# Row numbers of a counting stage in the result memory, node groups every three steps, and one-hot rows by ScalarE

## The chip, the cores and the metric

The kernel runs on one core of one Trainium2 chip. The metric is the device time of one execution in microseconds; every number below is of this core. Its engines are TensorE (matrix products, into a result memory of eight banks of 512 float32 values per partition), VectorE, ScalarE, GpSimd (here mostly the issuer of indirect DMAs, gathers and scatters by row number) and SyncE (the issuer of the plain DMAs).

## The reference

Four graph layers run one after another on the same 50,000 nodes of 128 features and 25,000 edges (`src`, `dst`, `dst` sorted), each followed by a residual and a layer norm:

```python
x = _layernorm(x + _L0_gnn_ref(x, node_vec, edge_weight, edge_attr_128, ...))   # attention with time encoding
x = _layernorm(x + _L1_gnn_ref(x, L1_gnn_W1, ...))      # two hidden convolutions and an output one
x = _layernorm(x + _L2_gnn_ref(x, edge_attr_128, src, dst, ...))    # two layers with edge rows and a mean
x = _layernorm(x + _L3_gnn_ref(x, edge_attr_2, src, dst, ...))      # attention over edges, two features
```

A convolution gathers `h[src]`, scales, adds up over equal `dst`, and multiplies by a 128x128 weight. An edge's sums only reach its own `dst`; a node without an incoming edge gets dense work alone (products, layer norms), which needs no gather. The result is a float32 table of 50,000 x 128.

## The kernel before

The edges are put in slots: 196 tiles of 128 (`TILES`), taken in 49 groups of four tiles (`GROUPS`, K = 4, G = 512). The 50,000 nodes are 98 groups of 512. The program is a sequence of blocks; each block has one list of instructions per engine, all engines meet at its end, and inside it only semaphores order them. The blocks that matter here:

1. **Counting** (L292 to L372). GpSimd issues 196 gathers of one tile each (L324: rows of x with one more value) into a ring of six, and SyncE writes each finished group to `xs0_d`. Beside it, with no semaphore between the two, VectorE makes one-hot rows by comparing the row of numbers 0 to 390 (`lanes`) with each edge's node number split in a low part (128 values) and a high part (391 values): four `tensor_tensor` operations a group in `equal` (L356 to L366), two of 128x512 and two of 128x1564. TensorE multiplies low and high one-hots into two banks `c_ps`, which are counts per node. The block ends when both strands have.
2. **Table and ranking** (to about 740 us): a short block turns counts into start positions, then each edge gets its slot, with 196 scatters (L528).
3. **Attention of layer 0**, and **the dense stage** (L1571 on, 107 steps): groups 0 to 48 are edge groups, then `NN` node groups. `dense_pe`, `dense_act` and `dense_dve` take each group through a pipeline of ten steps. GpSimd looks up 196 tiles of a table meanwhile, spread evenly over the steps, after VectorE's signal of each step.
4. **Four convolution blocks** (`conv_hidden` twice, the third convolution, `conv_edges`), with 55, 55, 57 and 54 steps (`STEPS_H`, `STEPS_T`, `STEPS_E`); a step takes a group of 512 edges: four gathers (L1919), scaling, a transpose, the segmented scan (L1938), products, and stores. In these blocks run also the **node passes**: the node groups 0 to `FILLED` - 1 are not in the dense stage but are done here, one pass after another, with instructions placed between those of the convolutions by a step counter T that runs on through all four blocks:

```python
FILLED = (2 * STEPS_H + STEPS_T + STEPS_E - 22) // 4 + 1
def node_of(T, phase):
    j, late = divmod(T - phase, 4)
    return j if late == 0 and 0 <= j < FILLED else -1
```

A pass has phases -3 to 21: load of x (-3), transpose of x (0), copy (1), product (2), squares (3), first root (4), y (5), transpose of y (7), copy (8), products (9, 12), and so on to the second norm (14, 16, 17, 19, 20) and the store (21). `fill_sp`, `fill_pe`, `fill_act_early`, `fill_act` and `fill_dve` issue them. The two transposes share the bank `fa_ps`.

5. **Fifth convolution** (`conv_edges` with `final`): 60 steps, no passes.
6. **Last one-hot rows** (L2521 on): SyncE broadcasts 49 rows of 512 lane numbers into a ring of six (`lane_b`); VectorE compares each with the partition's own number (L2591), TensorE multiplies the one-hots of a tile by a 128x196 table, VectorE picks one value a row (L2597). Then short work in rows, and the last block with the scatter of the results.

## Time and profile before

| | us |
|---|---|
| median of 3 runs | 4391.33 |
| their range | 4370.59 to 4411.52 |
| the profiled execution | 4386.8 |
| its span, first to last instruction | 4385.1 |

The median and the profiled execution are different executions of the same program. Times of the trace count from the span's start. Engines in the rows: PE is TensorE's products, PEld its weight loads, DVE VectorE, ACT ScalarE, POOL GpSimd; a q behind a name is that engine's sequencer. The buffer number is left out of a name, so `xs` stands for `xs0`, `x_f` for several tiles, `c_ps` for two banks.

### The profile page before, as it was taken

The numbers are of one execution on the slowest core, as the hardware profiler recorded it, in microseconds if no ns is written. First come the engines' busy times: TensorE is split into PE (matmuls) and PEld (weight loads), VectorE is DVE, ScalarE is ACT, GpSimd is POOL, SyncE is SP. The second block draws the span as 40 slices with busy tenths as digits, with TensorE's granted clock in tenths as the row PEclk, the third lists the DMA queues.
The fourth block names the chain that finished last, engine by engine and source line by source line (L and its number), as shares of the span: only waits on it lengthen the run. The fifth ranks groups of instructions, "written<-read, shape, count | busy, mean of one in ns | idle before, by whom it ended". The sixth has DMA issues, their size and how long they took to land. (4 is left out here: it accounts for less than half of the span.)

```text
span 4385.1 us, 57861 instructions
## 1 busy us (share of the span) xinstructions
PE 2745.6 (63%) x14955; PEld 2056.1 (47%) x14955; DVE 2776.3 (63%) x7991; ACT 1897.4 (43%) x5652; POOL 2119.6 (48%) x1978
## 2 busy tenths in 40 slices
PE   4514875599677776896467567555646646778422
PEld 1102443366355555674355456433445546776321
DVE  8914997344597999996245455566735436778533
ACT  0001332377323666797355355455734435660111
POOL 8874554566001222332755566455265545630466
PEclk7656998699799888998788777777767777888555
DMA  2233554677297444332355466555555556753221
GB/s 59 58 92 104 152 154 131 162 245 240 78 326 241 135 135 135 95 102 93 115 160 167 153 193 203 174 179 183 161 173 178 176 184 190 230 160 121 72 72 59
DMA packets 532622, 662.42 MB, mean 151 GB/s; under 512 B 99720, under 2 KB 300998, under 8 KB 532296
## 3 DMA queue, kind: packets, MB, share of 16 engines
q1 hardware_dynamic: 466440, 557.83, 40.2%
q0 software_dynamic: 65856, 100.90, 8.7%
q8 instruction: 125, 2.05, 0.2%
q14 instruction: 201, 1.65, 0.1%
HBM read 441.09 MB, written 246.14 MB: 157 GB/s over the span
## 5 line engine op out<-in xcount | busy, mean ns | idle before, releaser
L1919 POOL DMA_INDIRECT xg_c<-r_d,src_row x392 | 417.2, 1064 | 304.2 <-issue 114.8
L1593 POOL DMA_INDIRECT look<-table_d,ids x196 | 196.7, 1004 | 720.1 <-DVEq L1569 689.6
L324 POOL DMA_INDIRECT xs<-in_x_vec,node_i x196 | 294.2, 1501 | 61.1 <-issue 61.1
L1938 DVE TENSOR_TENSOR_SCAN agg_t_c<-flags_c,agg_t_c,t_ps_c 128x512 f32<-128x512 bf16 x144 | 183.6, 1275 | 191.9 <-remote 182.8
L2666 POOL DMA_INDIRECT out<-x_f,out_row x196 | 196.8, 1004 | 221.7 <-DVE x_f L2732 162.0
L1919 POOL DMA_INDIRECT xg_c<-x2d_d,src_row x196 | 198.6, 1013 | 215.9 <-DMA xg_c<-x2s_d 158.2
L528 POOL DMA_INDIRECT rows_d<-row,slot_i x196 | 194.7, 993 | 190.0 <-DVEq L590 142.3
L1919 POOL DMA_INDIRECT xg_c<-x1d_d,src_row x196 | 206.2, 1052 | 166.0 <-DMA xg_c<-x1s_d 107.1
L1919 POOL DMA_INDIRECT xg_c<-g1d_d,src_row x196 | 201.6, 1029 | 160.7 <-DMA xg_c<-g1s_d 100.3
L903 POOL DMA_INDIRECT xd<-in_x,ids x196 | 205.4, 1048 | 104.1 <-issue 52.9
L1998 PE MATMUL m_ps_c<-w_L_gnn_Wr,term_t_c 128*128 128x128 f32 x784 | 129.7, 318 | 200.8 <-issue 111.0
L1938 DVE TENSOR_TENSOR_SCAN agg_t_c<-flags_c,agg_t_c,term_t_c 128x512 f32<-128x512 bf16 x96 | 122.9, 1281 | 208.9 <-remote 139.9
L1998 PEld LDWEIGHTS m_ps_c<-w_L_gnn_Wr,term_t_c 128*128 128x128 f32 x784 | 114.5, 224 | 212.7 <-issue 117.1
L2683 PE MATMUL f_ps<-e2n,mean_in 2*128 2x128 f32 x392 | 97.5, 430 | 158.5 <-DVE y_f L2716 120.0
L623 PE MATMUL a_ps<-run,lo_t 128*128 128x391 f32 x392 | 175.5, 530 | 2.4
L359 DVE TENSOR_TENSOR hot_hi<-lanes,part_f 128x1564 bf16<-128x1564 f32 x98 | 174.3, 1779 | 0.0
L633 ACT ACT_TABLE_LOAD x1 | 1.3, 1283 | 387.1 <-PEq L399 387.1
L2683 PEld LDWEIGHTS f_ps<-e2n,mean_in 2*128 2x128 f32 x392 | 86.6, 324 | 169.5 <-issue 168.0
L2324 PE MATMUL z_ps_c<-w_L_gnn_W,agg_t_c 128*128 128x128 f32 x784 | 131.8, 307 | 52.8 <-issue 52.2
L1051 DVE SCALAR_TENSOR_TENSOR prod_t<-kv_ps,b_k,q_t 128x512 f32<-128x512 f32 x49 | 36.8, 751 | 193.2 <-issue 97.2
L2321 PE MATMUL z_ps_c<-w_L_gnn_W,own_t_c 128*128 128x128 f32 x784 | 136.1, 315 | 33.0 <-issue 32.5
L2017 ACT COPY term_t_c<-t_ps_c 128x512 f32<-128x512 f32 x98 | 57.1, 583 | 228.5 <-remote 203.4
(478 smaller groups left out, 9253.4 us busy)
## 6 DMA issues: line engine op xcount, KB each, us to landing
flags_c<-cont_d SPq DMA_DIRECT2D x245, 128.0 KB
xm<-rows_d SPq DMA_DIRECT2D x49, 512.0 KB
m_d<-m_c SPq DMA_DIRECT2D x98, 256.0 KB
r_d<-r_c SPq DMA_DIRECT2D x98, 256.0 KB
m_in_c<-m_d SPq DMA_DIRECT2D x98, 256.0 KB
e_c<-rows_d SPq DMA_DIRECT2D x98, 256.0 KB
x_f<-in_x SPq DMA_DIRECT2D x50, 256.0 KB
out<-x_f SPq DMA_DIRECT2D x50, 256.0 KB
```

The source lines that it names most:

```text
L324: pool.indirect_dma_start(out=xs0[:, h, k, :], out_offset=None, in_=a["x_vec"][:, :], in_offset=bass.IndirectOffsetOnAxis(ap=node_i[:, 1, ...
L359: return dve.tensor_tensor(to, number[:, 0:width].unsqueeze(1).to_broadcast([P, K, width]), same, ALU.is_equal)
L528: pool.indirect_dma_start(out=rows_d[:, :], out_offset=bass.IndirectOffsetOnAxis(ap=slot_i[:, h, k:k + 1], axis=0), in_=row[:, h, k, :], i ...
L623: pe.matmul(a_ps[u % 2][:, 0:HI], lo_t[:, u % 3, :], run[:, u % 3, :], start=True, stop=True).then_inc(based.sem, 1)
L903: pool.indirect_dma_start(out=xd[:, s, k, :], out_offset=None, in_=a["x"][:, :], in_offset=bass.IndirectOffsetOnAxis(ap=ids[:, 1, t:t + 1] ...
L1593: pool.indirect_dma_start(out=look[:, t, :], out_offset=None, in_=table_d[:, :], in_offset=bass.IndirectOffsetOnAxis(ap=ids[:, 0, t:t + 1] ...
L1919: pool.indirect_dma_start(out=xg[:, s, k, :], out_offset=None, in_=table, in_offset=bass.IndirectOffsetOnAxis(ap=src_row[:, t:t + 1], axis=0),
L1938: dve.tensor_tensor_scan(agg_t[:, n % 2, :], flags[:, n % SL, :], terms, agg_t[:, (n - 1) % 2, G - 1:G] if n else 0.0, ALU.mult, ALU.add). ...
L1998: mm = pe.matmul(m_ps[:, chunk(k)], term_t[:, n % 2, chunk(k)], weights[w_side][:, :], start=True, stop=True)
L2321: pe.matmul(z_ps[n % 2][:, chunk(k)], own_t[:, n % 3, chunk(k)], weights[w_own][:, :], start=k == 0, stop=False, skip_group_check=True)
L2666: pool.indirect_dma_start(out=out[:, :], out_offset=bass.IndirectOffsetOnAxis(ap=out_row[:, t:t + 1], axis=0), in_=x4[:, n % SF, k, :], in ...
L2683: mm = pe.matmul(f_ps[n % 3][:, chunk(k)], mean_in[:, n % SF, chunk(k)], e2n[:, :], start=True, stop=True)
```

## The change

Three parts. In the counting stage a bank `lanes_ps` of the result memory gets a copy of the numbers 0 to 390, and the four comparisons of a group read that in place of `lanes`. Node passes begin every three steps, not four, so `FILLED` grows and `NN` shrinks by the same number; some buffers of a pass get one more slot, two rows of x are loaded at step 0, waits on earlier passes are set accordingly, and in `fill_dve` phase 19 is placed ahead of phase 16 (both now fall into the same step). In the last one-hot stage ScalarE makes the rows, as |lane number - own number| and then relu(1 - that), and VectorE keeps only the picks.

```diff
+                lanes_ps = bank(ps, "lanes_ps")
...
                     dve.tensor_copy(lanes[:, :], lanes_i[:, :]).then_inc(steps_v.one(), 1)
+                    dve.tensor_copy(lanes_ps[:, 0:HI], lanes_i[:, :]).then_inc(steps_v.one(), 1)
...
                         same = part_f[:, s, t:t + K].unsqueeze(2).to_broadcast([P, K, width])
-                        return dve.tensor_tensor(to, number[:, 0:width].unsqueeze(1).to_broadcast([P, K, width]), same, ALU.is_equal)
+                        return dve.tensor_tensor(to, lanes_ps[:, 0:width].unsqueeze(1).to_broadcast([P, K, width]), same, ALU.is_equal)
...
-        FILLED = (2 * STEPS_H + STEPS_T + STEPS_E - 22) // 4 + 1
+        FILLED = (2 * STEPS_H + STEPS_T + STEPS_E - 22) // 3 + 1
...
-            y2_f = sb("y2_f", [P, 3, K, D], F32, st_f)
+            y2_f = sb("y2_f", [P, 4, K, D], F32, st_f)
-            u_f = sb("u_f", [P, 2, K, D], F32, st_f)
+            u_f = sb("u_f", [P, 3, K, D], F32, st_f)
-            rest_f = sb("rest_f", [P, 3, K], F32, st_f)
+            rest_f = sb("rest_f", [P, 4, K], F32, st_f)
...
-                j, late = divmod(T - phase, 4)
+                j, late = divmod(T - phase, 3)
...
-                j = 0 if T == 0 else max(node_of(T, -3), 0) if node_of(T, -3) > 0 else -1
-                if j >= 0:
+                for j in range(2) if T == 0 else range(node_of(T, -3), node_of(T, -3) + 1) if node_of(T, -3) > 0 else ():
...
-                    pe.wait_ge(f_xt.sem, f_xt.at(min(j + 2, FILLED)))
+                    pe.wait_ge(f_xt.sem, f_xt.at(min(j + 3, FILLED)))
...
-                    if j >= 2:
-                        pe.wait_ge(f_yt.sem, f_yt.at(j - 1))
+                    if j >= 3:
+                        pe.wait_ge(f_yt.sem, f_yt.at(j - 2))
...
+            apart_of = sb("apart_of", [P, 2, G], F32, st)
+            minus_lane = sb("minus_lane", [P, 1], F32, st)
...
-                            sp.wait_ge(hot_made.sem, hot_made.at(n - SZ + 1))
+                            sp.wait_ge(apart_made.sem, apart_made.at(n - SZ + 1))
...
                 def _(act):
+                    act.wait_ge(minus_ready.sem, minus_ready.at(1))
+                    for it in range(GROUPS + 1):
+                        n = it
+                        if n < GROUPS:
+                            act.wait_ge(lane_in[n % SZ].sem, lane_in[n % SZ].at(n // SZ + 1))
+                            if n >= 2:
+                                act.wait_ge(hot_made.sem, hot_made.at(n - 1))
+                            act.activation(apart_of[:, n % 2, :], lane_b[:, n % SZ, :], ACT.Abs, bias=minus_lane[:, 0:1]).then_inc(apart_made.sem, 1)
+                        n = it - 1
+                        if 0 <= n < GROUPS:
+                            if n >= 3:
+                                act.wait_ge(picks.sem, picks.at(K * (n - 2)))
+                            act.wait_ge(apart_made.sem, apart_made.at(n + 1))
+                            act.activation(one_hot[:, n % 3, :], apart_of[:, n % 2, :], ACT.Relu, bias=ones[:, 0:1], scale=-1.0).then_inc(hot_made.sem, 1)
...
-                    for n in range(GROUPS + 1):
-                        if n < GROUPS:
-                            dve.wait_ge(lane_in[n % SZ].sem, lane_in[n % SZ].at(n // SZ + 1))
-                            if n >= 3:
-                                dve.wait_ge(picks.sem, picks.at(K * (n - 2)))
-                            dve.tensor_scalar(one_hot[:, n % 3, :], lane_b[:, n % SZ, :], lane[:, 0:1], None, ALU.is_equal).then_inc(hot_made.sem, 1)
-                        if n >= 1:
-                            for t in range((n - 1) * K, n * K):
...
+                    for t in range(TILES):
+                        dve.wait_ge(picks.sem, picks.at(t + 1))
```

## Rows read from the trace of the kernel before

**Rows 1.** The page, part 1: busy time, share of the span, instructions

```profile
PE 2745.6 (63%) x14955; PEld 2056.1 (47%) x14955; DVE 2776.3 (63%) x7991; ACT 1897.4 (43%) x5652; POOL 2119.6 (48%) x1978
```

**Rows 2.** Stretches: length, PE, PEld, DVE, ACT, POOL busy, PEclk, DMA share, GB/s

```profile
100.00:150.00 50.00, 27.39 (x87) 9.90 (x87) 50.00 (x44) 0.00 (x0) 43.30 (x23) 0.60 0.24 56
...
2068.00:2430.00 362.00, 219.14 (x1363) 177.66 (x1363) 152.04 (x340) 169.80 (x518) 206.25 (x196) 0.79 0.49 153
2430.00:2800.00 370.00, 238.58 (x1428) 193.30 (x1428) 203.68 (x469) 190.97 (x583) 227.69 (x210) 0.76 0.60 190
...
3175.00:3560.00 385.00, 232.49 (x1428) 202.18 (x1428) 183.01 (x384) 164.96 (x479) 198.46 (x196) 0.73 0.58 176
3560.00:3950.00 390.00, 256.86 (x1742) 242.99 (x1743) 240.25 (x781) 216.32 (x587) 201.62 (x196) 0.76 0.63 193
```

**Rows 3.** GpSimd in time, counting stage: start, duration, line, idle before

```profile
8.30 1.17 POOL L324 DMA_INDIRECT xs<-in_x_vec,node_i  x1 [1.73 <-issue]
...
100.95 1.99 POOL L324 DMA_INDIRECT xs<-in_x_vec,node_i  x1 [0.30 <-issue]
...
241.25 1.00 POOL L324 DMA_INDIRECT xs<-in_x_vec,node_i  x1 [0.30 <-issue]
...
360.88 1.00 POOL L324 DMA_INDIRECT xs<-in_x_vec,node_i  x1 [0.30 <-issue]
```

**Rows 4.** TensorE in time, first product of the block after counting

```profile
370.41 1.64 PE L414 MATMUL tot_ps<-count,ones 128*128 128x391 f32 x2 [127.81 <-PEq L292]
```

**Rows 5.** VectorE in time, counting stage, two successive wide one-hots

```profile
100.31 1.78 DVE L359 TENSOR_TENSOR hot_hi<-lanes,part_f 128x1564 bf16<-128x1564 f32 x1
...
102.61 1.78 DVE L359 TENSOR_TENSOR hot_hi<-lanes,part_f 128x1564 bf16<-128x1564 f32 x1
```

**Rows 6.** VectorE in time, dense stage, one node group to the next

```profile
1900.93 0.69 DVE L1485 TENSOR_TENSOR half_u<-nu_ps,lk_n 128x512 f32<-128x512 f32 x1
...
1901.74 0.69 DVE L1491 TENSOR_TENSOR u_n<-y_n,half_u 128x512 f32<-128x512 f32 x1
...
1906.22 0.69 DVE L1485 TENSOR_TENSOR half_u<-nu_ps,lk_n 128x512 f32<-128x512 f32 x1
```

**Rows 7.** A gather and a scan in time, first convolution

```profile
2238.53 1.93 POOL L1919 DMA_INDIRECT xg_c<-x1d_d,src_row  x1 [0.30 <-issue]
```

```profile
2238.37 1.28 DVE L1938 TENSOR_TENSOR_SCAN agg_t_c<-flags_c,agg_t_c,term_t_c 128x512 f32<-128x512 bf16 x1 [7.68 <-remote]
```

**Rows 8.** The page, part 5: the scatters of the ranking stage

```profile
L528 POOL DMA_INDIRECT rows_d<-row,slot_i x196 | 194.7, 993 | 190.0 <-DVEq L590 142.3
```

**Rows 9.** Groups of instructions, 2068 to 3560: busy us, mean ns, idle before

```profile
L1823 ACT ACTIVATE x_f<-u_f,shift_f,inv_f 128x128 f32<-128x128 f32 x200 | 82.5, 492 | 2.4 <-issue 1.2 <-DVE shift_f L1884 1.1
...
L1845 DVE SCALAR_TENSOR_TENSOR y_f<-fm_ps,inv_f,b_mid 128x128 f32<-128x128 f32 x200 | 56.3, 345 | 2.0 <-issue 0.3
...
L1876 DVE SCALAR_TENSOR_TENSOR sp_f<-mom_f,rest_f 128x4 f32<-128x4 f32 x50 | 8.1, 162 | 1.7
```

**Rows 10.** VectorE and TensorE in time, last one-hot stage

```profile
3990.77 0.49 DVE L2591 TENSOR_SCALAR one_hot<-lane_b,lane 128x512 f32<-128x512 f32 x1
3991.17 0.42 DVE L2597 SCALAR_TENSOR_TENSOR picked<-tile_no,src_tile,pz_ps 128x196 f32<-128x196 f32 x1
...
3991.74 1.56 PE L2553 MATMUL pz_ps<-attn_in,one_hot 128*128 128x196 f32 x8 [0.19 <-DVE picked L2597]
...
3992.52 0.49 DVE L2591 TENSOR_SCALAR one_hot<-lane_b,lane 128x512 f32<-128x512 f32 x1
```

**Rows 11.** ScalarE in time, first convolution: a square from SBUF

```profile
2250.03 0.65 ACT L1800 ACTIVATE sq_f<-y_f 128x512 f32<-128x512 f32 x1
```

**Rows 12.** ScalarE in time, third convolution: two successive copies of x

```profile
3034.07 0.59 ACT L1784 COPY xt_f<-fa_ps 128x512 f32<-128x512 f32 x1 [9.99 <-remote]
...
3063.63 0.58 ACT L1784 COPY xt_f<-fa_ps 128x512 f32<-128x512 f32 x1 [10.10 <-remote]
```

**Rows 13.** Waits, fifth convolution (3570 to 3950): us, times, longest

```profile
POOL xg_c L1919 <- DMA xg_c<-g1s_d: 69.9, 16, 14.1
```

More of the change, by code:

```diff
@@ L365, in _ @@
                         for s, low in ((0, low_of[:, t:t + K, :]), (1, hot_lo[:, h:h + K, :])):
-                            equal(low, lanes, P, 2 * s, t)
-                            equal(hot_hi[:, s, h:h + K, 0:HI], lanes, HI, 2 * s + 1, t).then_inc(hot_ready.sem, 1)
+                            equal(low, P, 2 * s, t)
+                            equal(hot_hi[:, s, h:h + K, 0:HI], HI, 2 * s + 1, t).then_inc(hot_ready.sem, 1)
                     dve.wait_ge(hot_used.sem, hot_used.at(TILES))
@@ L1822, in fill_act @@
                     for k in range(K):
-                        made = act.activation(x4_f[:, j % 2, k, :], u_f[:, j % 2, k, :], ACT.Identity,
+                        made = act.activation(x4_f[:, j % 2, k, :], u_f[:, j % 3, k, :], ACT.Identity,
                                               bias=shift_f[:, j % 2, k:k + 1], scale=inv2_f[:, j % 2, k:k + 1])
@@ L1862, in fill_dve @@
                     dve.tensor_tensor(flat(half_f[:, :, :]), fn_ps[:, :], flat(lk_f[:, :, :]), ALU.max).then_inc(f_halved.sem, 1)
[L1863 to L1864 removed]
+                    if j >= 3:
+                        dve.wait_ge(f_rows.sem, f_rows.at(j - 2))
                     dve.wait_ge(f_halved.sem, f_halved.at(j + 1))
[L1866 removed]
+                    dve.tensor_tensor(u_f[:, j % 3, :, :], y2_f[:, j % 4, :, :], half_f[:, :, :], ALU.add).then_inc(f_u.sem, 1)
                     dve.wait_ge(f_u.sem, f_u.at(j + 1))
                     for k in range(K):
[L1869 to L1876 removed]
+                        dve.bn_stats(stats_f[:, k, :], u_f[:, j % 3, k, :]).then_inc(steps_v.one(), 1)
                 j = node_of(T, 19)
@@ L1884, in fill_dve @@
                     dve.scalar_tensor_tensor(shift_f[:, j % 2, :], mom_f[:, j % 2, :, 0], -1.0, inv2_f[:, j % 2, :], ALU.mult, ALU.mult).then_inc(f_shift.sem, 1)
+                j = node_of(T, 16)
+                if j >= 0:
+                    settled(dve)
+                    for k in range(K):
+                        dve.bn_aggr(mom_f[:, j % 2, k, :], stats_f[:, k, :]).then_inc(steps_v.one(), 1)
+                    settled(dve)
+                    dve.scalar_tensor_tensor(sp2_f[:, :], mom_f[:, j % 2, :, 1], 1.0 + EPS, rest_f[:, j % 4, :], ALU.mult, ALU.add).then_inc(f_spread_2.sem, 1)
             def all_filled(sp):
```

38 lines of the change are left out of this document (14 added, 24 removed).

## The prediction

> **What bounds the kernel now.** The program is a row of blocks with a barrier between them, and VectorE's 63% of the span [rows 1] mixes them; so I read the stages in order of time and asked of each which engine ends it. The view of stretches [rows 2] gives VectorE 50.00 us of 50 in the counting stage (100 to 150), but that stage does not end with VectorE: GpSimd's 196 gathers start at 8.30 and the last at 360.88, and TensorE's next block only begins at 370.41 [rows 3, 4]. While VectorE runs its one-hot operations a gather lasts 1.99 us and its start-to-start time is that of one pair of them (102.61 less 100.31, 2.30 us); once VectorE is done the same gather lasts 1.00 [rows 3, 5]. From 241.25 to 360.88 there are 92 steps, 1.300 us each. So GpSimd, slowed by VectorE, sets the end of this stage. The dense stage, in its part on node groups, is a VectorE cycle of 5.29 us a group (1906.22 less 1900.93) [rows 6]. In the convolution stages no engine is full: VectorE is busy 42, 55 and 48% of the first, second and fourth (2068 to 2430, to 2800, 3175 to 3560) [rows 2]. The stage of the last one-hot rows is VectorE's: 1.75 us a group of four tiles, from 3990.77 to 3992.52 [rows 10].
>
> **Part 1: row numbers in the result memory.** The 196 operations of L359 read two tensors of SBUF now, `lanes` and `part_f`; afterwards one of SBUF and one of TensorE's result memory. Is that what holds the gathers? The scan L1938 of the first convolution also reads two SBUF tensors, and the gather that starts beside it takes 1.93 us [rows 7]. In the ranking stage (392 to 740) VectorE is busy too, with operations that read at most one SBUF tensor (L550, L563), and there 196 scatters take 993 ns each [rows 8]. I take the ranking stage as the nearer case, since each comparison will have one SBUF source, too. Then gathers follow at 1.300 us from the first: 8.30 + 195 x 1.300 = 261.8 in place of 360.88, and what follows the last gather (9.5 us to 370.41) stays. Gain: 99 us. VectorE's own work ends near 242 (98 pairs of 2.30 us are 225), under the new end at 262: it would matter only if a pair grew beyond about 2.5 us. The nearest row with a source in the result memory, L1485 (`half_u<-nu_ps,lk_n`), takes 0.69 us for 512 elements, and L1491 with both in SBUF 0.69 [rows 6]: I take 0, with 0.06 us an operation as the upper end, 12 us in all, still hidden. The added copy of 391 numbers is under 1 us of VectorE, hidden too. Bounds for the part: 0 and 99 us.
>
> The Trainium skill, SBUF — State Buffer, section "Who interferes with whom", says that a VectorE instruction with one SBUF input, outside the two-port modes, does not contend with GpSimd, and one with two does, with GpSimd's reads: the trace agrees (1.99 against 1.00 us). But the same section infers that `tensor_tensor` does not stall descriptor generation, since that needs the write interface; by that rule the part would bring nothing and the sum below would lose its 99 us. The 2.30 us lockstep speaks against it.
>
> **Part 2: node passes every three steps.** (2x55+57+54-22) = 199; 199//4+1 = 50 passes become 199//3+1 = 67. So 17 node groups leave the dense stage, whose node groups fall from 48 to 31, and 17 enter the convolutions. Leaving is worth 17 x 5.29 = 90 us: each is a full turn of the VectorE cycle, nothing hides it. The 196 table look-ups are spread over 79 steps, not 96: 2.5 x 1.30 = 3.2 us a step, inside 5.29.
>
> Entering: one pass costs VectorE 6.15 us (13 rows of the grouped view from 56.3 to 8.1 us for 50 passes, 307.5 together; ScalarE's work is of the same size, the largest row 82.5) [rows 9], beside two transfers of 256 KB. Fully exposed on VectorE that would be 17 x 6.15 = 105 us. How much of added work shows? From the first convolution stage to the second, VectorE's work grows by 51.6 us and the stage by 8; from the fourth to the fifth by 57.3 us of VectorE, 51.3 of ScalarE and 24.4 of TensorE, and the stage by 5 [rows 2]. That is 0.09 to 0.16 us of time per us of VectorE, 9 to 17 us here. I take 35, twice that and more, because a pass is now three steps apart and its chain is tighter: TensorE's turn of y waits for ScalarE's copy of x made in the same step (before, two steps earlier), with the next step's z, m and term matmuls queued behind it; VectorE's phase 19 stands before phase 16 and waits for a root taken one step before, with the next scan behind it; and phases 5, 11 and 14 fall into one step. SyncE issues two more DMAs a pass, in a queue that also carries the gathers' base rows. Bounds for the cost: 0 and 105. Net: -90 + 35 = -55 us.
>
> **Part 3: last one-hot rows by ScalarE.** VectorE's step of 0.40 us (3990.77 to 3991.17) goes, 49 times: 19.6 us. Next late is one of three. VectorE itself: 1.75 - 0.40 = 1.35 us a group. TensorE: eight records within 1.56 us, the last overlapping the next group: 1.3 to 1.4 us [rows 10]. ScalarE: two operations; the nearest row, a square of 512 elements from SBUF without a pointer bias, takes 0.65 us [rows 11], and 128 elements with scale and bias from pointers take 0.49 [rows 9]; neighbours overlap a little, and Abs waits for the Relu just issued: 1.25 to 1.45 us a group. I take 1.40: 49 x 0.35 = 17 us, plus 1 us because the first rows are ready before VectorE is. Bounds 14 and 21. ScalarE is idle there, only Exp is queued behind, and SyncE's ring of six waits for Abs, earlier than now.
>
> The Trainium skill, ScalarE: Activation LUTs, "Rules for kernel authors", advises VectorE for relu-like operations. Here one VectorE operation (0.49 us) becomes two of ScalarE, so the rule holds for work and not for the bound engine; the same page's pace (280 ns with a pointer bias, 0.833 ns an element, 93 ns of overlap) gives an estimate of 1.23 us a group for the two, by which VectorE's 1.35 would be the bound and the saving 20 us.
>
> **The sum**, against the profiled execution's own 4386.8 us (span 4385.1; 4.5 below the median 4391.3): 4386.8 - 99 - 55 - 18 = 4214.8. I write 4215.
>
> **Rivals.** (A) *The gathers stay at 1.99 us*: what holds them is VectorE's writing or its occupation, not the second read. Against: [rows 8]. 4386.8 - 55 - 18 = 4314. Chance 0.07. (It is also what the Trainium skill's SBUF — State Buffer, "Who interferes with whom", infers for `tensor_tensor`.) (B) *Each pass brings a stall of its own.* In the third convolution ScalarE waits 10.1 us at L1784, the copy of x that a pass makes, and did so 29.6 us before, one pass earlier [rows 12]. If that wait belongs to the pass, a pass costs it and its own work, 10.1 + 5.3 [rows 6] = 15.4 us. Only there (5 more passes, the other 12 at 2 us): 101 us, and 4386.8 - 99 - 90 + 101 - 18 = 4281; chance 0.14. In all four stages: 17 x 15.4 = 262, 4386.8 - 99 - 90 + 262 - 18 = 4442, slower; it decides from 12.2 us a pass on (207/17). Chance 0.03. Against both: the fifth convolution carries no pass, and its gathers wait for transfers just so, 16 times, up to 14.1 us [rows 13]. (C) *The convolutions swallow the passes*: 4386.8 - 99 - 90 - 18 = 4180. It is one end of my forecast; with a faster end still (nothing in the rows promises one) chance 0.13.
>
> **How the numbers follow.** The forecast (cost of the passes 10 to 70 us) runs from 4190 to 4250, chance 0.63. Adding C (to 4180) and B in the third stage gives 0.90; 3 us on either side for part 3, and 7 because single runs of the kernel lie 20 us to either side of the median, make 4170 to 4290; A and the slow end of B are left out. This kernel's measurement tells about 1% (44 us) from no change. Faster by over 1% holds in the forecast, in C, in B for one stage and in A: with some allowance 0.95. Within 1% 0.02; slower 0.03.
>
> **What would show it.** Step 1: gathers at L324 of 1.0 us from the first, the last near 262, TensorE's block at 271, VectorE's pair still 2.30. If it is false they stay at 2.0. Step 2: the dense stage ends 90 us sooner relative to its start, with the same 5.3 us a node group; the four convolution stages together are 35 us longer, VectorE's work in them up by 105; if B is right ScalarE's waits at L1784 grow in number with the passes. Step 3: a group of four tiles in 1.40 us, VectorE no longer waiting on a one-hot of its own. The prediction fails if the passes cost over 100 us, or if a source in the result memory makes VectorE's pair longer than 2.5 us.

## The result, and the profile after

The changed kernel takes 4413.0 us, the kernel before 4394.1 (medians of 20 runs each): ratio 1.0045, 95% interval 1.0027 to 1.0062. The forecast was 4215, 4170 to 4290. The profiled execution of the changed kernel has a span of 4409.5 us against 4385.1; so 24 us have to be accounted for where a gain of 172 was forecast.

From one stage's first gather (or first product) to the next one's, before and after:

| stretch | before | after | forecast |
|---|---|---|---|
| start to the ranking stage's first product | 396.1 | 464.3 (+68.2) | -99 |
| ranking, attention | 994.9 | 1000.6 (+5.7) | 0 |
| dense stage | 678.2 | 600.4 (-77.8) | -90 |
| convolutions, to the last scan | 1859.9 | 1905.8 (+45.9) | +35 |
| last scan to the final scatters | 163.5 | 145.9 (-17.6) | -18 |
| final scatters | 292.4 | 292.5 | 0 |

One line is off by 167 us and no other by more than some 12. The loss is in the counting stage. Stretches of the changed kernel, columns as in [rows 2]; the second is the dense stage:

```profile
100.00:150.00 50.00, 7.96 (x23) 2.57 (x21) 9.36 (x8) 0.00 (x0) 38.42 (x39) 0.50 0.38 99
1465.00:2017.00 552.00, 416.59 (x2479) 331.41 (x2479) 499.53 (x1737) 376.73 (x1374) 196.97 (x196) 0.89 0.37 119
2065.00:2428.00 363.00, 241.77 (x1483) 195.48 (x1483) 173.05 (x422) 191.17 (x597) 212.55 (x196) 0.80 0.49 159
2428.00:2800.00 372.00, 253.93 (x1526) 204.35 (x1527) 222.93 (x559) 208.30 (x646) 209.11 (x198) 0.80 0.55 182
```

Between 100 and 150 us VectorE, full before, is busy 9.36 us of 50; GpSimd makes 39 gathers where it made 23. In the first two convolution stretches, as long as before, VectorE has 21 and 19 us more to do, the passes. The gathers do what was forecast: GpSimd in time, start, duration and line, answers to [rows 3].

```profile
94.28 1.00 POOL L325 DMA_INDIRECT xs<-in_x_vec,node_i  x1 [0.30 <-issue]
95.58 1.00 POOL L325 DMA_INDIRECT xs<-in_x_vec,node_i  x1 [0.30 <-issue]
...
262.43 1.00 POOL L325 DMA_INDIRECT xs<-in_x_vec,node_i  x1 [0.30 <-issue]
```

They last 1.00 us at one per 1.30, and the last starts at 262.43 (forecast 261.8). VectorE in time, answers to [rows 5]:

```profile
94.81 0.69 DVE L361 TENSOR_TENSOR low_of<-lanes_ps,part_f 128x512 bf16<-128x512 f32 x1 [17.76 <-remote]
95.42 1.78 DVE L361 TENSOR_TENSOR hot_hi<-lanes_ps,part_f 128x1564 bf16<-128x1564 f32 x1
97.11 0.68 DVE L361 TENSOR_TENSOR hot_lo<-lanes_ps,part_f 128x512 bf16<-128x512 f32 x1
97.71 1.78 DVE L361 TENSOR_TENSOR hot_hi<-lanes_ps,part_f 128x1564 bf16<-128x1564 f32 x1
117.23 0.69 DVE L361 TENSOR_TENSOR low_of<-lanes_ps,part_f 128x512 bf16<-128x512 f32 x1 [17.75 <-issue]
```

A pair still takes 2.29 us (97.71 less 95.42): the source in the result memory costs nothing. But after the two pairs of a group VectorE stands for 17.7 us. It waits there for `hot_used`: the buffers have room for two groups, so TensorE must be through with the last but one. TensorE in time, end of one group and the next:

```profile
79.04 0.53 PE L381 MATMUL c_ps<-hot_hi,hot_lo 128*128 128x391 bf16 x1
...
97.25 0.51 PE L381 MATMUL c_ps<-hot_hi,low_of 128*128 128x391 bf16 x1 [17.68 <-DVE hot_hi L361]
99.55 0.51 PE L381 MATMUL c_ps<-hot_hi,hot_lo 128*128 128x391 bf16 x1 [1.78 <-issue]
...
101.15 0.53 PE L381 MATMUL c_ps<-hot_hi,low_of 128*128 128x391 bf16 x1
101.48 0.53 PE L381 MATMUL c_ps<-hot_hi,hot_lo 128*128 128x391 bf16 x1
119.68 0.51 PE L381 MATMUL c_ps<-hot_hi,low_of 128*128 128x391 bf16 x1 [17.66 <-DVE hot_hi L361]
```

By its records TensorE is through with one group at 79.5 us and with the next at 102, and waits for VectorE. But VectorE, whose wait at 117.23 is for the first of the two, is let go 38 us after its last record. Both can't be right; the ends of products are modelled, and the event is what counts: in the trace TensorE's reports, one a tile, rise some 5.6 us apart where this goes on, and 0.3 to 0.7 us apart in a group of the kernel before. The waits of VectorE to 300 us (us, times, longest), and TensorE's next block, which answers to [rows 4]:

```profile
DVE low_of L361 <- remote: 140.5, 9, 17.8
DVE low_of L361 <- issue: 53.2, 3, 17.7
```

```profile
438.62 1.64 PE L416 MATMUL tot_ps<-count,ones 128*128 128x391 f32 x2 [1.62 <-PEq L292]
```

Twelve waits, 193.7 us, all before 284 us; from there VectorE takes 2.3 us a pair again until 434. They do not end with the gathers but 20 us later. The last gather ends at 263.4, the last transfer of the stage at 267, and VectorE still has these two, in time:

```profile
273.33 0.69 DVE L361 TENSOR_TENSOR low_of<-lanes_ps,part_f 128x512 bf16<-128x512 f32 x1 [17.02 <-remote]
...
283.14 0.69 DVE L361 TENSOR_TENSOR low_of<-lanes_ps,part_f 128x512 bf16<-128x512 f32 x1 [5.13 <-remote]
```

"remote" is the name that the view of waits gives to a release for which it finds no work that ended then. There is no other core here.

The last one-hot stage answers to [rows 10]; VectorE in time:

```profile
4030.23 0.41 DVE L2609 SCALAR_TENSOR_TENSOR picked<-tile_no,src_tile,pz_ps 128x196 f32<-128x196 f32 x1
...
4031.59 0.41 DVE L2609 SCALAR_TENSOR_TENSOR picked<-tile_no,src_tile,pz_ps 128x196 f32<-128x196 f32 x1
```

These two are four picks apart: 1.36 us a group, picks back to back. So it goes for some 22 groups; from about 4045 us on a group takes 1.43, and that is ScalarE's pace, in time:

```profile
4061.41 0.72 ACT L2575 ACTIVATE apart_of<-lane_b,minus_lane 128x512 f32<-128x512 f32 x1
4062.03 0.70 ACT L2581 ACTIVATE one_hot<-apart_of,ones 128x512 f32<-128x512 f32 x1
4062.83 0.72 ACT L2575 ACTIVATE apart_of<-lane_b,minus_lane 128x512 f32<-128x512 f32 x1
```

In the dense stage node groups take longer than before [rows 6]; two of them, VectorE in time:

```profile
1977.15 0.69 DVE L1487 TENSOR_TENSOR half_u<-nu_ps,lk_n 128x512 f32<-128x512 f32 x1
...
1982.84 0.69 DVE L1487 TENSOR_TENSOR half_u<-nu_ps,lk_n 128x512 f32<-128x512 f32 x1 [0.55 <-ACT lk_n L1459]
```

5.69 us, and 5.7 to 6.5 for 21 of the 31 node groups in a row, where it was 5.3.

### The profile page after: what moved, and what is told of

It is laid out like the page before. It is cut to its first block and busy times, and to the rows that moved or that the text cites. A ratio compares the mean times of both kernels' runs of the same rounds, so it can differ in the third digit from the quotient of the medians.

```text
span 4409.5 us, 57770 instructions
## 1 busy us (share of the span) xinstructions
PE 2750.2 (62%) x14819; PEld 2064.3 (47%) x14819; DVE 2773.0 (63%) x7978; ACT 1960.9 (44%) x5767; POOL 2018.6 (46%) x1978
## 5 line engine op out<-in xcount | busy, mean ns | idle before, releaser
L1920 POOL DMA_INDIRECT xg_c<-r_d,src_row x392 | 405.6, 1035 | 334.1 <-issue 126.2
L381 PE MATMUL c_ps<-hot_hi,low_of 128*128 128x391 bf16 x196 | 97.8, 499 | 218.8 <-DVE hot_hi L361 112.1
L325 POOL DMA_INDIRECT xs<-in_x_vec,node_i x196 | 195.8, 999 | 61.0 <-issue 61.0
L361 DVE TENSOR_TENSOR hot_hi<-lanes_ps,part_f 128x1564 bf16<-128x1564 f32 x98 | 174.1, 1777 | 0.0
L361 DVE TENSOR_TENSOR low_of<-lanes_ps,part_f 128x512 bf16<-128x512 f32 x49 | 33.4, 682 | 193.7 <-remote 140.5
```

Of the source, the lines that this page charges most:

```text
L325: pool.indirect_dma_start(out=xs0[:, h, k, :], out_offset=None, in_=a["x_vec"][:, :], in_offset=bass.IndirectOffsetOnAxis(ap=node_i[:, 1, ...
L361: return dve.tensor_tensor(to, lanes_ps[:, 0:width].unsqueeze(1).to_broadcast([P, K, width]), same, ALU.is_equal)
L1920: pool.indirect_dma_start(out=xg[:, s, k, :], out_offset=None, in_=table, in_offset=bass.IndirectOffsetOnAxis(ap=src_row[:, t:t + 1], axis=0),
```

## The experiments

Each group of runs was made on one chip, beside runs of the kernel before on the same chip. Those came out at two levels, with nothing between: 4363 to 4419 us (the comparison above and runs 5 to 15) and 3923 (runs 1 to 4 and 16 to 18). What differs between the levels is the finding of this study (what sets a level isn't known), so each run says at which it was: "late" for the first, "prompt" for the second.

| run | level | this | before | ratio, 95% interval |
|---|---|---|---|---|
| 1 part 1 | prompt | 3824.6 | 3923.4 | 0.9751, 0.9734 to 0.9767 |
| 2 part 2 | prompt | 3855.3 | 3923.4 | 0.9845, 0.9819 to 0.9870 |
| 3 part 3 | prompt | 3905.9 | 3923.4 | 0.9954, 0.9938 to 0.9971 |
| 4 part 1, one report a group | prompt | 3824.0 | 3923.4 | 0.9752, 0.9736 to 0.9769 |
| 5 all three | late | 4374.7 | 4362.9 | 1.0032, 1.0008 to 1.0057 |
| 6 all three, one report a group | late | 4375.9 | 4362.9 | 1.0024, 1.0000 to 1.0047 |
| 7 part 1, gathers paced (flawed) | late | 4516.7 | 4377.6 | 1.0341, 1.0281 to 1.0402 |
| 8 part 1, split products | late | 4474.4 | 4377.6 | one run |
| 9 part 1, short rows | late | 4448.3 | 4377.6 | one run |
| 10 parts 2 and 3 | late | 4312.7 | 4377.6 | 0.9860, 0.9805 to 0.9916 |
| 11 part 1, one gather per 1.87 us | late | 4383.9 | 4419.1 | 0.9932, 0.9907 to 0.9957 |
| 12 part 1, one gather per 2.5 us | late | 4408.1 | 4419.1 | one run |
| 13 part 1, one gather per 1.57 us | late | 4357.1 | 4407.3 | 0.9887, 0.9841 to 0.9932 |
| 14 before, convolutions paced | late | 4249.9 | 4407.3 | 0.9630, 0.9582 to 0.9678 |
| 15 all three, counting at 1.87 | late | 4320.0 | 4407.3 | 0.9779, 0.9723 to 0.9835 |
| 16 all three, all paced | prompt | 4037.8 | 3923.8 | 1.0287, 1.0270 to 1.0304 |
| 17 the same, longer pauses | prompt | 4176.8 | 3923.8 | 1.0642, 1.0625 to 1.0660 |
| 18 all three, counting at 1.57 | prompt | 3789.2 | 3922.6 | 0.9665, 0.9649 to 0.9681 |

**Runs 1 to 3: each part alone.** The edits are the three parts of the diff.

> Part 1 alone. In the changed kernel the gathers end at 263 us, as forecast, but VectorE waits for TensorE's reports (hot_used) eleven or twelve times up to 17.8 us while the gathers run, and the counting strand ends at 437 us in place of 242. Theory L (the gathers at their full pace of 1.30 us make TensorE late, whatever else was changed): the same here, stages after it move by 68 us, and the kernel takes 4394 + 68 = 4462 us. Rival M (the loss of the changed kernel comes from parts 2 or 3 or from their sum): part 1 alone saves the forecast 99 us, 4295.

> Part 2 alone. By the two traces the dense stage gets 79 us shorter and the five convolutions 46 us longer. If the parts are independent: 4394 - 79 + 46 = 4361 us, with VectorE's counting work unchanged (2.30 us a pair). Rival B of the prediction (each pass brings a wait of its own of some 10 us) would give 4394 - 90 + 262 = 4566; the rival that the convolutions swallow the passes, 4304.

> Part 3 alone. Forecast: 1.40 us a group of four tiles in place of 1.75, 18 us less: 4376 us. Rival: ScalarE's two operations bind at 1.45 us or more and its start is late, so that 10 us or less are saved: 4384 or more.

Part 1 alone saves 98.8 us, where L had a loss of 68 and M a gain of 99. But the kernel before takes 3923 us here, 470 less than where the changed kernel had been compared, so this does not decide between them; run 9 does. The profile of run 1, GpSimd, VectorE and TensorE in time:

```profile
261.99 0.99 POOL L325 DMA_INDIRECT xs<-in_x_vec,node_i  x1 [0.30 <-issue]
```

```profile
98.12 1.77 DVE L361 TENSOR_TENSOR hot_hi<-lanes_ps,part_f 128x1564 bf16<-128x1564 f32 x1
99.81 0.68 DVE L361 TENSOR_TENSOR hot_lo<-lanes_ps,part_f 128x512 bf16<-128x512 f32 x1
100.41 1.77 DVE L361 TENSOR_TENSOR hot_hi<-lanes_ps,part_f 128x1564 bf16<-128x1564 f32 x1
```

```profile
271.51 1.64 PE L416 MATMUL tot_ps<-count,ones 128*128 128x391 f32 x2 [29.30 <-PEq L292]
```

The same instructions, the same gathers at 1.30 us, and no wait at all: TensorE's block starts at 271.51, where the forecast had 271. Parts 2 and 3 save 68.1 and 17.4 us here (forecast 55 and 18). By stages, run 2 against run 3 (which leaves the dense stage and the passes alone): dense 583.4 against 677.6, or against 675.6 in run 1, so -92 to -94; convolutions 1462.2 against 1439.4 (run 3) and 1443.7 (run 1), so +19 to +23.

Where are the 470 us? Against run 3 the kernel before of [rows 2] takes 1859.9 against 1439.4 us in the convolutions, 594.6 against 579.9 in the attention stage, and 292.4 against 271.5 in the final scatters, while ranking and dense stages agree within 3 us. So the difference sits in the stages with many gathers beside TensorE's work. The waits, us, times and longest, of the kernel before in its convolutions (2069 to 3929):

```profile
DVE agg_t_c L1938 <- remote: 322.8, 38, 43.3
ACT term_t_c L2017 <- remote: 203.4, 30, 23.0
ACT xt_f L1784 <- remote: 161.4, 23, 24.9
```

and those of run 1 in its own (1945 to 3388), none of which is put down to "remote":

```profile
ACT term_c L2035 <- DMA xg_c<-x1d_d,src_row: 115.2, 40, 14.0
ACT term_c L2035 <- DMA xg_c<-r_d,src_row: 102.2, 40, 9.4
```

```profile
DVE agg_t_c L1940 <- ACT term_t_c L2019: 84.3, 25, 19.6
```

Over the whole span the kernel before has 175 waits for "remote", 1204 us in sum (1053 of them in the four convolutions with passes, 129 in the final scatters, 3.7 in the ranking stage), the changed kernel 199 with 1255 us; run 1 has none. All three that are shown wait for TensorE, the scan in part through ScalarE's copy. Counting in the traces how long after a product's record its semaphore rises: in the kernel before 56% of TensorE's reports in the convolutions come over 0.5 us late, in run 1 2%.

One more thing differs, and nothing here explains it. The traces at the late level hold fewer of the semaphores' rises: 40,000 in the kernel before, 37,600 to 40,600 in the changed kernel and runs 5 to 13 and 15, and 52,300 in run 14, against 82,600 to 84,100 in each trace at the prompt level. The programs ask for the same; what is missing is mostly from the stages with many gathers (in the four convolutions 13,500 of the 39,400 that run 1 has). So a share of late reports at the late level is rough: of TensorE's 1018 reports in the convolutions of the kernel before, 886 have left a rise. And since every run on record carries a profile, it stays open whether the recording has a part in the late level itself.

**Run 4: one report a group**, on top of part 1; **runs 5 and 6**: the changed kernel again, and with the same edit.

```diff
-                            dve.wait_ge(hot_used.sem, hot_used.at((g - 1) * K))
+                            dve.wait_ge(hot_used.sem, hot_used.at(g - 1))
...
-                        mm.then_inc(hot_used.sem, 1)
+                        if t % K == K - 1:
+                            mm.then_inc(hot_used.sem, 1)
```

> Part 1 alone, but TensorE reports once for a group of four tiles (after its eighth product) in place of once a tile; VectorE waits for the same progress. Theory U (the reports are what is late: while the gathers run one gets through per 5.6 us): 1 report per 4.60 us of VectorE's work is needed, so the strand loses at most 1.0 us a group while the gathers last, 45 groups, and ends near 290 us in place of 437; the kernel takes about 4394 + 68 - 147 = 4315 us. Theory X (TensorE's instructions themselves are slow, 5.6 us for the two products of a tile): nothing changes, 437 us and 4462.

Run 4 came out at the prompt level, where U and X say the same; it tells nothing.

> The changed kernel itself once more. The first four experiments ran on a chip on which the kernel before takes 3923 us, not 4394, and on which TensorE's reports come at once under gathers at 1.30 us. Theory S (two sorts of chip, or states of one: where the reports under gathers are late, the counting part loses; where they are prompt, it gains 99 us): if the kernel before takes about 3923 here, the three savings add up, 99 + 68 + 17 = 184, and this kernel takes 3739; if it takes about 4394 here, this one takes 4413 again, with eleven waits of 17.7 us in VectorE's counting work. Rival I (the parts disturb each other, and that is why all three together lost): 3923 or more with the kernel before at 3923.

> The changed kernel, with TensorE's report of the counting stage given once for a group of four tiles in place of once a tile. On a chip with late reports theory U (a report gets through once per 5.6 us) gives a counting strand that ends near 290 us and 4413 - 147 = 4266 us; theory X (TensorE's instructions themselves are slow there) gives 4413, unchanged. On a chip with prompt reports both give the time of the changed kernel.

Both at the late level. Run 5 repeats the first comparison: twelve waits of up to 17.7 us, 1.0032. Run 6 has a quarter of the reports and the same waits, VectorE to 300 us:

```profile
DVE low_of L361 <- remote: 121.9, 8, 17.7
DVE low_of L361 <- issue: 70.9, 4, 17.7
```

So theory U is out: a quarter of the reports changes nothing, and what is slow is TensorE's own progress. One group, eight products, per 22.4 us (117.23 less 94.81) is 2.80 us for a product with its weight load, where the records say 0.33 (101.48 less 101.15).

**Run 7: a pause after each gather**, with an edit that missed.

```diff
                                 bounds_check=N - 1, oob_is_err=False).then_inc(xs0_in[h].sem, 16)
+                            if t < 112:
+                                pool.wait_ge(steps_g.sem, steps_g.so_far())
+                                pool.memset(idle[:, :], 0.0).then_inc(steps_g.one(), 1)
```

> Part 1 alone, and GpSimd clears 700 unused values per partition (about 0.7 us) after each of the first 112 gathers, so that these follow at about 2.0 us, not 1.30, while TensorE has products to make. On a chip with late reports, theory G (TensorE advances in the gaps that GpSimd leaves between two gathers, whatever VectorE does): TensorE keeps up, VectorE no longer waits for it and ends near 242 us, the gathers end at 8 + 112 x 2.0 + 84 x 1.3 = 341 us, and the kernel takes about 20 us less than before. Rival V (TensorE is slow because VectorE reads the result memory while gathers run): VectorE waits as in the changed kernel, and the strand ends near 430 us. On a chip with prompt reports both give 20 us less than before.

VectorE's wait for the row numbers counts GpSimd's steps and now took in all 112 clearings. Its waits:

```profile
DVE lanes L351 <- POOL idle L332: 204.7, 1, 204.7
DVE low_of L365 <- remote: 51.8, 3, 17.7
```

It began at 222 us, beside gathers without pauses, and had the waits of 17.7 us again. Of these 84 gathers at 1.30 us the last starts at 326.23, and VectorE's last wait ends 9 us later:

```profile
335.00 0.69 DVE L365 TENSOR_TENSOR low_of<-lanes_ps,part_f 128x512 bf16<-128x512 f32 x1 [16.32 <-remote]
```

The question stayed open.

**Runs 8 and 9: what the 2.80 us goes by.** Run 8 makes each product in two; run 9 gathers 16 values of a row.

```diff
-                            mm = pe.matmul(c_ps[s][:, 0:HI], low, hot_hi[:, s, t % 8, 0:HI],
-                                           start=(t == 0), stop=(t == TILES - 1))
+                            for a0, a1 in ((0, 196), (196, HI)):
+                                mm = pe.matmul(c_ps[s][:, a0:a1], low, hot_hi[:, s, t % 8, a0:a1],
+                                               start=(t == 0 and a0 == 0), stop=(t == TILES - 1 and a1 == HI))
```

```diff
-                                out=xs0[:, h, k, :], out_offset=None, in_=a["x_vec"][:, :],
+                                out=xs0[:, h, k, 0:16], out_offset=None, in_=a["x_vec"][:, :],
```

> Part 1 alone, each product of 391 columns made as two of 196 and 195 (the same sums). On a chip with late reports: if what is slow is each instruction of TensorE, the 5.6 us of a tile double to about 11, and VectorE gets a group ahead only every 45 us while gathers run; if the time goes by columns or by the reports of a tile, it stays at 22.4 us a group. On a chip with prompt reports the counting stage ends at 262 us in both.

> Part 1 alone; the gathers of the counting stage take only the first 16 values of each row in place of 129 (as many rows and transfers, an eighth of the bytes; the attention stage gets incomplete rows). On a chip with late reports: theory D (GpSimd's writing of the transfers' descriptors holds TensorE): nothing changes, 22.4 us a group and 437 us. Rival W (the bytes that arrive in SBUF hold it): the waits go and the strand ends at 242 us.

VectorE in time in run 8, three groups on:

```profile
124.85 0.69 DVE L361 TENSOR_TENSOR low_of<-lanes_ps,part_f 128x512 bf16<-128x512 f32 x1 [40.11 <-remote]
...
169.66 0.69 DVE L361 TENSOR_TENSOR low_of<-lanes_ps,part_f 128x512 bf16<-128x512 f32 x1 [40.12 <-remote]
...
214.46 0.69 DVE L361 TENSOR_TENSOR low_of<-lanes_ps,part_f 128x512 bf16<-128x512 f32 x1 [40.12 <-issue]
```

44.8 us a group: twice 22.4, for twice the instructions and the same columns. TensorE's time goes by its instructions, 2.80 us for a weight load and its product, of 391 columns or of 196. Nor is it the clock. The granted clock of the stage (100 to 240 us) is 0.50 in the changed kernel, the lower level of 1.2 GHz, and a mix of both levels in run 1 (0.57 to 0.64); but in run 1 reports rise 0.65 us a tile apart where it is 0.50 (111 to 114 us) and 0.33 where it is 1.00 (125 to 127), not 5.6. Run 9, with an eighth of the bytes, has the waits of run 6 almost to the digit:

```profile
DVE low_of L361 <- remote: 121.6, 8, 17.7
DVE low_of L361 <- issue: 70.9, 4, 17.7
```

So rival W is out; what holds TensorE goes with the gathers as such, not with their data. Run 9 is also part 1 alone at the late level: 71 us more than the kernel before (one run), where theory L had 68 and M a gain of 99. L holds there.

**Run 10: parts 2 and 3 without part 1.**

> Parts 2 and 3 without part 1. On a chip with late reports the traces of before and after give -79 + 46 - 18 = -51 us, 4394 - 51 = 4343 (or 4363 - 51 = 4312 where the kernel before takes 4363). On a chip with prompt reports 68 + 17 = 85 us less than 3923. Rival: where TensorE's reports are late, the closer passes lose what the dense stage gains, and the kernel is within 20 us of before.

-64.9 us, a little more than the sum of the stages (-51). At the late level these two parts pay. By stages: dense 598.1 (678.2 in the kernel before, 679 to 681 in runs 7 to 9), convolutions 1892.0. And with the comparisons' two sources in SBUF as before, gathers follow at 2.30 us and no one-hot waits for TensorE, at the same late level.

**Runs 11 to 13: the pause, mended.** The wait now counts GpSimd's steps as they were before the first gather; clearings of 700, 1500 and 350 values.

> The paced gathers again, now with VectorE waiting for the row numbers alone (in the paced kernel before, its first comparison waited for all 112 clearings, until 222 us, so that nothing was paced while TensorE worked). A gather and its clearing take 1.87 us, so the first 124 end at 240 us and the last of 196 at 334. On a chip with late reports, theory G (TensorE is slow only beside the writing of a gather, 1.0 of each 1.87 us, and is at its own pace in the gaps): VectorE waits little, its strand ends by 290 us, and the kernel takes 20 to 30 us less than before. Rival R (a TensorE product takes 2.80 us whenever gathers are about, whatever the gaps): 17.7 us waits until 334 us, and the strand ends near 470. On a chip with prompt reports both give 27 us less than before.

> The same with clearings of 1500 values after each of the first 90 gathers: one gather per 2.6 us, the last at 380 us. Theory G: no waits for TensorE at all, VectorE ends at 242 us. Rival R: 17.7 us waits until the last gather. If the slowing goes by the share of time that gathers are written, VectorE's waits are a third or less of those at 1.87 us.

> Part 1 with a shorter clearing (350 values, about 0.4 us) after each of the first 160 gathers: one gather per 1.57 us in place of 1.87, the last at 8 + 160 x 1.57 + 36 x 1.30 = 306 us. On a chip with late reports: if the gap alone protects TensorE (theory G with any gap above the 0.3 us of the plain sequence), VectorE waits little, the block ends near 315 us and the kernel takes 50 to 60 us less than before. If the change from 17.7 us waits (1.30) to none (1.87) is gradual, VectorE waits somewhere between, and the strand ends between 260 and 400 us. On a chip with prompt reports: 55 us less.

GpSimd in run 13, in time:

```profile
100.43 1.00 POOL L328 DMA_INDIRECT xs<-in_x_vec,node_i  x1 [0.16 <-issue]
101.44 0.40 POOL L334 MEMSET idle<- 128x350 f32 x1
102.01 1.00 POOL L328 DMA_INDIRECT xs<-in_x_vec,node_i  x1 [0.16 <-issue]
```

and what VectorE waits for there up to 300 us:

```profile
DVE count L378 <- PE c_ps L386: 2.6, 1, 2.6
```

None of the three has a wait of a one-hot, at a level where one gather per 1.30 us had twelve. VectorE's last one-hot begins at 240, 244 and 239 us, the last gather ends at 335, 374 and 309, and the kernel takes 35, 11 and 50 us less than before. A pause of 0.41 us between two gathers (0.57 in all, in place of 0.30) is the whole difference between 2.80 us a product and full pace. Rival R falls, and so does rival V of run 7, since VectorE reads the result memory here too. What theory G forecast came true, and the change between the two is not gradual down to 1.57 us; what lies between 1.57 and 1.30 was not tried.

G's reason, that TensorE advances in the gaps between two gathers, does not fit, though. The kernel before has the same gap of 0.30 us after each gather of 1.99 [rows 3] and no waits, and at one per 1.30 TensorE stays slow when no gather is made any more. What fits better is a pace: counted from the first gather at 1.30 us to the last wait's end it is 275 us for 196 gathers (8.2 to 283.1) and 118 for the 84 of run 7 (217.3 to 335.0), 1.40 us a gather in both, as if something took 1.40 us for each and worked off what had piled up. Then 1.30 is too fast and 1.57 is not. That is an estimate from these two cases, and no run names the something.

**Run 14: the same pause in the convolutions of the kernel before**, and nothing else.

```diff
                             bounds_check=bound - 1, oob_is_err=False).then_inc(c_gathered[s].sem, 16)
+                        pool.wait_ge(steps_g.sem, steps_g.so_far())
+                        pool.memset(idle_c[:, :], 0.0).then_inc(steps_g.one(), 1)
```

> The kernel before, with a clearing of 350 values after each gather of the five convolution stages and nothing else. There 84% of the gathers follow each other at 1.30 us, and most of TensorE's reports behind three of them are late. Theory G: with 1.57 us between gathers the reports are prompt, the convolution stages (about 1860 us together where the kernel before takes 4380, about 1430 where it takes 3923) get 100 to 300 us shorter on a chip with late reports. Rival: the late reports there come from the stages' other transfers, and the pauses only lengthen the stages or leave them as they are. On a chip with prompt reports the pauses lengthen them by up to 196 x 0.27 = 53 us a stage, since 4 x 1.57 = 6.3 us is more than its step of 5.5.

-157.4 us, by adding work. The convolutions take 1721.6 us in place of 1859.9, and no wait in them is put down to "remote" any more; the scan, which had waited 322.8 us for it, now waits as in run 1:

```profile
DVE agg_t_c L1941 <- ACT term_t_c L2020: 152.9, 36, 21.5
```

The convolutions are still 280 us longer than at the prompt level without pauses (1439 to 1444), but this is what the pauses themselves cost: runs 16 and 18 differ by 249 us there at the prompt level (1717.9 against 1468.6), and 980 gathers x 0.27 us are 265. Run 14 at the late level and run 16 at the prompt one (with 17 more passes) take nearly the same in the convolutions. The share of late reports of 0.33 on which the expectation of run 17 rests is not to be trusted: only 627 of TensorE's 1018 reports there have left a rise, and a report without one is easily taken for late. Of the rises that are in the trace 3% came over 0.5 us late, in the kernel before 49%. So the pause takes most of the lateness here, too.

**Runs 15 and 18: all three parts with the counting stage paced; runs 16 and 17: the convolutions paced too.**

> All three parts, with the clearing of 700 values after each of the first 124 gathers of the counting stage. The savings found so far should add up: 27 us (pacing with part 1) and 65 (parts 2 and 3 on a chip with late reports), 92 us less than the kernel before; on a chip with prompt reports 27 + 85 = 112 us less. Rival (what is saved ahead of the convolutions is lost in them, as their start shifts): 65 us or less.

> All three parts, clearings of 350 values after the first 160 gathers of the counting stage and after every gather of the convolutions. If the savings add up: 50 us (part 1, paced), 65 (parts 2 and 3), 157 (convolutions paced) = 272 us less than the kernel before on a chip with late reports, and 4407 becomes 4135. Rival (the passes every three steps fill what the pauses free, so that the two gains overlap): 200 us less.

> The same with 500 values (about 0.53 us, one gather per 1.70 us) in the convolutions. A step's four gathers then take 6.8 us, against 6.3. With 0.4 us pauses a third of TensorE's reports there are still late (0.33, from 0.56): if longer pauses make more of them prompt, 20 us or more less than with 350; if the four gathers themselves bind by now, 49 x 0.5 = 25 us a stage more, 100 us in all.

> All three parts, clearings of 350 values after the first 160 gathers of the counting stage, no pauses elsewhere. Where TensorE is late under gathers (the kernel before at 4340 to 4420): 50 + 65 = 115 us less than before. Where it is prompt (before at 3923): 52 + 85 = 137 us less, 3786. Rival where it is late: what is saved ahead of the convolutions is partly lost in them, as in the run with longer pauses (87 saved of 92), so 105 us.

Run 15 (late): -87.3 us where 92 was the sum. Run 18 (prompt): -133.4 where 137 was, and 3789 for a forecast of 3786. The savings add up once TensorE isn't held. Runs 16 and 17 met the prompt level, and there the pauses in the convolutions only cost: 248.6 us between runs 16 and 18, and another 139 for the longer ones, 128 of them in the convolutions (980 gathers x 0.13 us are 127: the four gathers of a step bind). What they give with the three parts at the late level was not measured. All three parts with pauses in the counting stage alone beat the kernel before at either level (run 15 with clearings of 700, run 18 with 350), and the changed kernel at the late one; the changed kernel was not run at the prompt level, where the savings of runs 1 to 3 add up to 184 us, 51 more than run 18 has.

## Why the prediction was wrong

**Part 1, the step that failed.** Its first half held: one source in SBUF lets the gathers go at 1.300 us from the first (262.43 for 261.8), the result memory costs VectorE nothing, and at the prompt level the 99 us came in full (98.8, run 1). What failed is "VectorE's own work ends near 242, under the new end at 262: it would matter only if a pair grew beyond about 2.5 us". The strand has two engines, and the step costed one. TensorE's products are not mentioned in it; at the late level they take 2.80 us each while gathers follow at 1.30 (runs 5, 6, 8, 9), 22.4 us a group against VectorE's 4.6. The pair did not grow; it waited. The strand did 10 of its 98 pairs by 38 us, 22 more until 283, and the other 66 after that, and ended at 437, not 242: +67 in place of -99. In the kernel before the comparisons with two SBUF sources held the gathers at one per 2.30 us, and that slow pace protected TensorE, whose reports came within 0.1 us of the record; runs 11 to 13 protect it with pauses instead. The change took away a delay that something else lived on. The bounds of the part, 0 and 99, excluded a loss without a reason for it.

The Trainium skill, SBUF — State Buffer, "Who interferes with whom", was right for this case in what contends (two SBUF inputs do, one does not) and its inference that `tensor_tensor` leaves descriptor generation alone was not: run 1 changes only where one source lies, and the gather goes from 1.99 to 1.00 us. Rival A had that inference with a chance of 0.07; it did not happen.

**What the rows had already shown.** [Rows 7] and [rows 12] carry the mark: waits of 7.68 and 10 us "<-remote" on a program of one core. The prediction took those of ScalarE as a question of whose they are, a pass's or the transfers', and set rival B by it. They were TensorE's late progress beside gathers at 1.30 us (run 14, with pauses, has none of them in the convolutions); there and in the final scatters the kernel before had it all along, nearly all of its 1204 us of such waits. A look at where gathers at 1.30 us and TensorE's work already met would have warned of the loss, if not priced it: that pair of conditions was new to the counting stage, not to the kernel. The stage that the prediction took as its nearer case, the ranking, is one of scatters, and they hardly showed it (one wait, 3.7 us).

**Part 2.** -90 + 35 was forecast; -77.8 + 45.9 measured at the late level, -93 and +21 at the prompt one. The 5.29 us a node group is as good as exact where TensorE is prompt (5.5). Where it is late, 21 node groups take 5.7 to 6.5 us, which is the 12 us that the gain lacks. The likely reason is that 196 look-ups on fewer steps stand closer (2.5 a step); no run tests it. A pass costs 42 us / 17 = 2.5 us at the late level (mean of five traces with passes every three steps, 1896.9, less that of seven without convolution edits and with every four, 1855.1) and 21 / 17 = 1.2 at the prompt one. The traces of either kind spread over some 40 us (1882.0 to 1921.5 and 1835.6 to 1877.0), so the first figure is good to about 1 us a pass. The forecast's 35 lies between 21 and 42; neither B (15.4 a pass) nor C holds. Of the 35 the part below 17 us was read from rows and the part above was caution; the rows' 0.09 to 0.16 us a VectorE us were too low even for the prompt level, where it is 0.2 (19 to 23 us for 105).

**Part 3.** -18 forecast, -17.6 in the trace, -17.4 in run 3. The 1.40 us a group was right on average, as two of the three candidates bind in turn: VectorE at 1.36 us a group for the first half, while ScalarE's lead lasts, and then ScalarE at 1.43. From the first pick to the last it is 69.7 us in place of 86.1, 16.4 less, and the first pick comes 1.6 us sooner after the last scan; in run 3 a group takes 1.41 on average. The prediction's estimate of 1.23 us for ScalarE's two operations had neighbours overlap: they don't here, each waits for the one before it. ScalarE's Relu takes 0.71 us, more than the 0.65 of [rows 11]; the figure from the Trainium skill, ScalarE: Activation LUTs, "What ACT_TABLE_LOAD costs" (280 ns with a pointer bias and 0.833 ns an element, an estimate of 0.71 for 512), is what the trace has.

**Sum.** The stages add up to the difference of the spans: 68.2 + 5.7 - 77.8 + 45.9 - 17.6 + 0.1 = 24.5 us more, against 172 less forecast; 167 of the 196 between them are part 1. That parts 2 and 3 came out near their terms is for part 3 the mechanism too; for part 2 it is in part luck, since 35 us was a guess between what the two levels show, made without knowing of them.

**What stays open.** Whether the level belongs to a chip or to a state it is in. All runs of a group agree, and each of the seven groups was at one level or the other as a whole. The record numbers their chips 8, 7, 12, 11, 0, 0 and 6. Number 0 stands there twice, late in runs 13 to 15 and, seven minutes later, prompt in runs 16 and 17. If it is the same chip, the level is a state; whether the number means the same one isn't on record. Also open is what couples a software gather to TensorE's instructions, why 0.27 us more between gathers undoes it, and whether the recording of the profile has a part in it, as the missing rises suggest it might; no run without recording is on record.

## What to carry to other kernels

Before a slow transfer issuer is sped up, ask which engines run beside it in that stage and whether they have been seen beside it at the new pace elsewhere in the trace; a strand has every engine of its ring in it, and each needs its rate. A wait put down to "remote" in a program of one core is a lead, not a remainder: sum such waits by stage and look for what they coincide with. And where a kernel's time has two levels, as here, an edit is judged at both levels: closer gathers in the counting stage gain 99 us or lose some 70, pauses in the convolutions gain 157 or cost some 250, and the three parts with a pause in the counting stage alone gain at both.

## What the runs showed of the hardware

- At the late level a TensorE weight load with its product takes 2.80 us while GpSimd issues gathers of 128 rows at one per 1.30 us, whatever its columns (391 or 196), the bytes gathered (516 or 64 a row) or the reports given (one a tile or one in four); at one per 1.57, 1.87, 2.30 or 2.5 us it is at full pace in this stage. It stays slow for some 16 us after the last transfer (267 to 283). At the prompt level 1.30 us costs nothing.
- In such a stretch the profile's records of products end long before VectorE is let go by them, 38 us here; the semaphore's rise tells when, where the trace has it.
- A `tensor_tensor` of VectorE with one source in the result memory and one in SBUF takes as long as with two in SBUF (1.78 us for 1564 elements) and leaves gathers at 1.00 us instead of 1.99.
- Work added to GpSimd, a clearing of 350 values after each gather of the convolutions, made a kernel 157 us faster at the late level (run 14); at the prompt level such clearings cost 249 us (runs 16 and 18).
